# Routed attention: two small subtractions of each group are issued by VectorE instead of GpSimd

## Chip, cores and metric
One core of a Trainium2 chip (trn2). The metric is the device time of one execution, in microseconds (us); the median of three executions of the kernel before is 633.46 us.

## What is computed
The reference is a chain of six layers on a tensor of 32 images, 32 channels, 16x16 points (as tokens: 32 sequences of 256 tokens of width 32): linear attention, a peripheral convolution, a linear transformer, a mixture of experts, a squared attention, and at the end the routed blocks, which alone are touched here:

```python
def step(h, p):
    op = jnp.argmax(h[0, 0, :NOPS])
    q = h @ p['wq'][op]
    k = h @ p['wk'][op]
    v = h @ p['wv'][op]
    attn = jax.nn.softmax(jnp.einsum('bqd,bkd->bqk', q, k) * scale, axis=-1)
    y = jnp.einsum('bqk,bkd->bqd', attn, v) @ p['wo'][op]
    h = jnp.where(p['am'][op], y, h)
    z = jax.nn.relu(h @ p['w1'][op] + p['b1'][op]) @ p['w2'][op] + p['b2'][op]
    h = jnp.where(p['fm'][op], z, h)
    return (h, None)
```

The first value of the state decides which of 19 operations a step takes, and whether the step has an attention, a feed-forward part, both or neither. With these inputs the program runs three attentions in this stage.

## The kernel before
The kernel is one hand-written program with a stream of instructions for each engine; semaphores order them, and no scheduler moves anything. Within a stream the instructions run in the order of the code. The last stage is `routed_blocks` (from line 1510). A loop runs the steps that do something; `body(p)` is one step on each engine, written twice with two sets of semaphores (`sets[p]`).

**The attention of one step.** The 32 sequences are worked on in G = 8 groups of J = 4 sequences, which lie side by side in the 128 partitions. For a group g TensorE makes the scores twice. `scores` (line 1643) makes them with queries in the partitions, so that VectorE can take the maximum over the keys (`maximum`, L2085): one reduction for two of the group's sequences (`pair(0)` lies in PSUM banks 2 and 3, `pair(1)` in banks 0 and 1), 128 partitions x 1024 values to 4. `turned` (L1657) makes them with keys in the partitions, and ScalarE takes their exponential (L1909). The softmax needs the maximum of each query subtracted, and in the turned layout a query is a column. So the maxima are turned as well and brought in by a matmul (`shift`, L1651).

**The split.** The maxima are fp32, and they are turned and brought in as bf16. To lose no precision they are split in three parts. `m.parts` holds for each query 32 fp32 columns; `m.upper` is the same memory seen as pairs of bf16, and its index 1 is the upper half of each fp32 value. Part 0 is the maximum itself, part 1 is part 0 minus its own upper half, part 2 is part 1 minus its upper half. These two subtractions of 128x8 values are `split(g)` (L1977 and L1979 on GpSimd). Behind them TensorE turns the upper halves of all three (`maxima`, L1673, two transposes into PSUM), VectorE copies the result (`copy_maxima`, L2091; for group 0 it is ScalarE, L1896), and `shift` takes it from there.

**What waits for what.** `split(g)` waits for both maxima of group g (semaphore `max_done`), and its second subtraction for the first (`parts`). TensorE's `maxima(g+1)` waits for both subtractions of its group and also for the first maximum of the group after it, `maximum(g+2, 0)`, since the transposes are written into bank 2, which that maximum reads.

**The order on TensorE**, for group g: `pair_turned(g, 0)` (with the scores of pair 0 of group g+2 in between), `values(g-1)` (L1703), `pair_turned(g, 1)` (with the scores of pair 1 of g+2), `maxima(g+1)`, `sums(g-1)` (L1712, the denominators).

**The order on VectorE**, for group g: `maximum(g+2, 0)`, `spread_inverses(g-2)` (L2103), `copy_maxima(g+1)` (L2091), `invert(g-1)` (L2096 and L2098, which wait for the sums), `maximum(g+2, 1)`. So the maximum of pair 1 of one group stands directly in front of the maximum of pair 0 of the next. Ahead of the loop stand the four maxima of groups 0 and 1.

**The order on GpSimd**, for group g: `add_halves(g-1, 1)` (L1993, adds two halves of the exponentials for the sums), `split(g+1)`, `add_halves(g, 0)`, `normalise(g-2)` (L1984).

Of the kernel before, what the change touches and what calls it, by code (L numbers as in the profile page):

```python
# [8 lines left out]
ALU = mybir.AluOpType  # L9
# [1500 lines left out]
def routed_blocks(nc, m, sem):  # L1510
# [40 lines left out]
    def pair(h):  # L1551

        return (2, 3) if h == 0 else (0, 1)

    def scored(g, h):

        return 2 * g + h + 1
# [37 lines left out]
    def registers(eng, name):  # L1595
        return [eng.alloc_register(f"{name}_{r}") for r in ("step", "op", "code")]

    with nc.Block() as block:
# [364 lines left out]
        @block.gpsimd  # L1963
        def _(pool):
            regs = registers(pool, "pool")
            pool.memset(m.parts[:, :, :, :, :], 0.0).then_inc(zeroed, 1)
            pool.wait_ge(zeroed, 1)

            def body(p):
                sg, old = sets[p], sets[1 - p]  # L1970

                def split(g):

                    part = [m.parts[:, g % 2, :, :, 3 * g + i] for i in range(3)]
                    upper = [m.upper[:, g % 2, :, :, 3 * g + i, 1] for i in range(2)]
                    pool.wait_ge(sg["max_done"], scored(g, 1))
                    pool.tensor_tensor(part[1], part[0], upper[0], ALU.subtract).then_inc(sg["parts"], 1)  # L1977
                    pool.wait_ge(sg["parts"], 2 * g + 1)
                    pool.tensor_tensor(part[2], part[1], upper[1], ALU.subtract).then_inc(sg["parts"], 1)  # L1979

                def normalise(g):

                    pool.wait_ge(sg["inv_done"], g + 1)
                    pool.tensor_tensor(h[:, g * N:(g + 1) * N], m.yz[:, g, 0:N], m.yz[:, g, N:2 * N],  # L1984
                                       ALU.mult).then_inc(sg["y_made"], 1)

                def add_halves(g, i):

                    pool.wait_ge(sg["exp_done"], J * g + 2 * i + 2)
                    if g >= 2:  # L1990
                        pool.wait_ge(sg["sums_ready"], g - 1)
                    two = slice(2 * i, 2 * i + 2)
                    pool.tensor_tensor(m.esum[:, g % 2, two, :], m.et[:, g % 2, two, 0:N], m.et[:, g % 2, two, N:2 * N],  # L1993
                                       ALU.add).then_inc(sg["halves_added"], 1)

                def attention():
                    split(0)
                    split(1)
                    add_halves(0, 0)
                    for g in range(1, G):  # L2000
                        add_halves(g - 1, 1)
                        if g + 1 < G:
                            split(g + 1)
                            add_halves(g, 0)
                        if g >= 2:
                            normalise(g - 2)
                    normalise(G - 2)

                pool.wait_ge(old["through"], 3)
                for name in NAMES:  # L2010
                    pool.sem_clear(old[name])
                pool.sem_inc(cleared, 1)
                with pool.If(pool.snap(regs[2]) > 1):
                    attention()
                with pool.Else():
                    pool.nop()
                state(pool, "pool", regs, 1 - p)

            state(pool, "pool", regs, 0)
            in_turns(pool, regs, body)  # L2020

        @block.vector
        def _(dve):
# [45 lines left out]
            def body(p):  # L2069
                sg = sets[p]  # L2070

                def attention():
                    dve.wait_ge(sg["mats_ready"], 1)
                    dve.scalar_tensor_tensor(m.sabd[:, :], ps[:, 0, 0:128], float(C) ** -0.5, m.blkone[:, :],
                                             ALU.mult, ALU.mult).then_inc(sg["mats_masked"], 1)
                    dve.tensor_tensor(m.vobd[:, :], ps[:, 1, 0:128], m.blkone[:, :], ALU.mult).then_inc(sg["mats_masked"], 1)
                    candidates()
                    dve.wait_ge(zeroed, 1)

                    def maximum(g, h_):  # L2080
                        a = pair(h_)[0]
                        dve.wait_ge(sg["s_ready"], scored(g, h_))
                        if g >= 2:
                            dve.wait_ge(sg["m_ready"], g - 1)
                        dve.tensor_reduce(m.parts[:, g % 2, :, a:a + 2, 3 * g].rearrange("p s i -> p i s"),  # L2085
                                          ps[:, a:a + 2, :].rearrange("p i (s m) -> p i s m", s=S),
                                          AXX, ALU.max).then_inc(sg["max_done"], 1)

                    def copy_maxima(g):
                        dve.wait_ge(sg["m_ready"], g + 1)  # L2090
                        dve.tensor_copy(m.mrow[:, g % 2, :], m_ps(g)).then_inc(sg["m_copied"], 1)  # L2091

                    def invert(g):

                        dve.wait_ge(sg["sums_ready"], g + 1)
                        dve.transpose(m.sumt[:, :], ps[:, 6, N:2 * N]).then_inc(sg["sums_turned"], 1)  # L2096
                        dve.wait_ge(sg["sums_turned"], g + 1)
                        dve.reciprocal(m.sinv[:, :], m.sumt[:, 0:N:32]).then_inc(sg["sums_inverted"], 1)  # L2098

                    def spread_inverses(g):  # L2100

                        dve.wait_ge(sg["sums_inverted"], g + 1)
                        dve.transpose(m.yz[:, g, N:2 * N].rearrange("p (b c) -> p b c", c=32),  # L2103
                                      m.sinv[:, :].unsqueeze(2).broadcast_to([128, N // 32, 32])).then_inc(sg["inv_done"], 1)
                        if g == G - 1:
                            dve.wait_ge(sg["inv_done"], g + 1)
                            dve.wait_ge(sg["y_kept"], g + 1)
                            dve.tensor_tensor(h[:, g * N:(g + 1) * N], m.yz[:, g, 0:N], m.yz[:, g, N:2 * N],
                                              ALU.mult).then_inc(sg["y_last"], 1)

                    for g in range(2):
                        for i in range(2):
                            maximum(g, i)
                    for g in range(G):
                        if g + 2 < G:
                            maximum(g + 2, 0)
                        if g >= 2:
                            spread_inverses(g - 2)
                        if g + 1 < G:
                            copy_maxima(g + 1)  # L2120
                        if g >= 1:
                            invert(g - 1)
                        if g + 2 < G:
                            maximum(g + 2, 1)
                    spread_inverses(G - 2)
                    invert(G - 1)
                    spread_inverses(G - 1)

                def feed_forward():
                    dve.wait_ge(sg["loaded"], 16 * NLOAD)  # L2130
                    dve.wait_ge(sg["first_ready"], 1)
                    choose(1 - p, row=ps[0:1, 7, 64:64 + NOPS], read=sg["first_read"])

                    def relu(r):
                        dve.wait_ge(sg["z1_ready"], r + 1)
                        if r >= 4:
                            dve.wait_ge(sg["z2_ready"], (r - 4) // 2 + 1)
                        dve.tensor_scalar(hidden_pair(r), ps[:, up_pair(r), :], m.b1[:, p:p + 1], 0.0, ALU.add,  # L2138
                                          ALU.max).then_inc(sg["relu_v"], 1)

                    for r in RELU_V:
                        relu(r)
                    state(dve, "dve", regs, 1 - p)

                with dve.If(dve.snap(regs[2]) > 1):
                    attention()
                with dve.Else():
                    candidates()
                with dve.If(dve.snap(regs[2]) < 3):
                    feed_forward()  # L2150
                with dve.Else():
                    dve.wait_ge(sg["y_made"], G - 1)
                    dve.wait_ge(sg["y_last"], 1)
                    choose(1 - p)
                    state(dve, "dve", regs, 1 - p)
                dve.sem_inc(sg["through"], 1)
# [527 lines left out]
```

## Time and profile before
| | us |
|---|---|
| median of 3 executions | 633.46 |
| lowest, highest | 630.22, 634.5 |
| the profiled execution | 627.3 |
| its span, from first to last instruction | 625.5 |
| VectorE busy | 407.7 |
| TensorE busy | 538.3 |
| GpSimd busy | 157.7 |

The rows further down come from the profiled execution. PE is TensorE (PEld its weight loads), DVE is VectorE, ACT is ScalarE, POOL is GpSimd. A row of the timeline gives the start in us from the span's start, the duration in us, engine, line, operation, what is written and read, shapes and count; in brackets how long the engine sat idle before it and which instruction ended that. R names a large tile in which nearly all buffers of this stage lie, and ps is PSUM. "issue" means that the profile shows nothing that the engine waited for.

### The profile page before, as it was taken

How to read it: one execution, taken by the hardware profiler on the slowest of the kernel's cores; microseconds unless marked ns; L12 is line 12 of the kernel's file. 1: busy time of each engine (PE TensorE's matmuls, PEld its weight loads, DVE VectorE, ACT ScalarE, POOL GpSimd, SP SyncE). 2: the span in 40 equal slices, each digit the busy share in tenths (PEclk: the TensorE clock that was granted, in tenths of full speed). 3: DMA queues.
4: the chain of work that ended last, by engine and by line, in shares of the span. 5: the costliest groups of instructions: out<-in, count | busy, mean ns of one | idle time of the engine just before them, and what ended most of it. 6: DMA issues, size and time to landing. Idle time of an engine off the chain costs nothing. (4 is left out here: it accounts for less than half of the span.)

```text
span 625.5 us, 15132 instructions
## 1 busy us (share of the span) xinstructions
PE 538.3 (86%) x6151; PEld 324.8 (52%) x6156; DVE 407.7 (65%) x756; ACT 300.1 (48%) x511; POOL 157.7 (25%) x209
## 2 busy tenths in 40 slices
PE   7966879989999888787888879689998999899983
PEld 3555644659998632264655544326552654265420
DVE  5769886862224698786888858635765575568453
ACT  4157543233221300257888854354655465656562
POOL 1024520000000000404665600001770276038400
PEclk9768999999788889897999999768999999999987
DMA  8400042000000290000000000000000000000002
GB/s 242 44 2 3 4 166 57 2 1 1 1 1 0 45 209 18 2 2 1 3 2 1 3 19 1 9 11 2 2 2 12 1 2 1 12 1 2 1 6 70
DMA packets 21794, 15.05 MB, mean 24 GB/s; under 512 B 17209, under 2 KB 20313, under 8 KB 21082
## 3 DMA queue, kind: packets, MB, share of 16 engines
q1 hardware_dynamic: 21722, 14.00, 9.2%
q8 instruction: 56, 0.92, 0.6%
q14 instruction: 16, 0.13, 0.1%
HBM read 8.71 MB, written 1.08 MB: 16 GB/s over the span
## 5 line engine op out<-in xcount | busy, mean ns | idle before, releaser
L1909 ACT ACTIVATE R<-ps 128x512 f32<-128x512 f32 x96 | 52.1, 594 | 41.3 <-PE ps L1657 41.3
L2085 DVE TENSOR_REDUCE R<-ps 128x4 f32<-128x1024 f32 x48 | 56.5, 1209 | 11.6 <-PE ps L1643 11.3
L1436 POOL TENSOR_TENSOR R<-R 128x512 f32<-128x512 f32 x32 | 45.3, 1417 | 47.5 <-DVE R L1370 47.5
L1993 POOL TENSOR_TENSOR R<-R 128x512 f32<-128x512 f32 x42 | 53.3, 1268 | 15.7 <-ACT R L1909 15.7
L1370 DVE TENSOR_TENSOR R<-ps,lasting 128x512 f32<-128x512 f32 x64 | 41.2, 687 | 13.9 <-PE ps L1302 13.9
L1657 PE MATMUL ps<-tmpA,R 32*128 32x256 f32 x384 | 49.2, 374 | 0.0
L1643 PE MATMUL ps<-R,tmpA 32*128 32x256 f32 x384 | 48.4, 408 | 0.0
L1403 ACT ACTIVATE R<-R 128x1536 f32<-128x1536 f32 x32 | 47.3, 1477 | 0.1
L1302 PE MATMUL ps<-R,Q 32*128 32x128 f32 (+1 forms) x512 | 31.2, 358 | 14.9 <-ACT R L1419 14.9
L1302 PEld LDWEIGHTS ps<-R,Q 32*128 32x128 f32 x512 | 25.3, 192 | 22.5 <-DVE R L1370 19.0
L1657 PEld LDWEIGHTS ps<-tmpA,R 32*128 32x128 f32 x384 | 36.3, 185 | 1.0
L1977 POOL TENSOR_TENSOR R<-R 128x8 f32<-128x8 f32 x24 | 5.0, 206 | 122.4 <-DVE R L2085 122.4
L1789 PE MATMUL ps<-R,early 32*128 32x512 f32 x160 | 34.7, 760 | 0.0
L1932 ACT ACTIVATE R<-ps,b 128x1024 f32<-128x1024 f32 x25 | 27.0, 1113 | 10.0 <-PE ps L1789 10.0
L1643 PEld LDWEIGHTS ps<-R,tmpA 32*128 32x128 f32 x384 | 29.6, 189 | 4.0 <-ACT tmpA L1888 3.5
L1419 ACT ACTIVATE R<-ps 128x256 f32<-128x256 f32 x64 | 24.3, 380 | 12.8 <-DVE R L1370 12.8
L1225 POOL MEMSET R<- 128x512 bf16 x1 | 0.5, 524 | 112.7 <-POOLq L915 112.7
L1329 PE MATMUL ps<-R 128*32 128x128 f32 (+1 forms) x512 | 27.9, 338 | 1.1 <-ACT R L1403 1.0
L2138 DVE TENSOR_SCALAR R<-ps,b 128x1024 f32<-128x1024 f32 x15 | 19.3, 1284 | 14.6 <-PE ps L1789 14.2
L1703 PE MATMUL ps<-R,Q 128*32 128x256 f32 x384 | 25.7, 385 | 2.0 <-ACT R L1909 2.0
L89 PE MATMUL ps<-lasting 128*128 128x512 f32 x40 | 22.8, 723 | 2.7 <-DVE R L154 2.7
L1827 PE MATMUL ps<-R,early 128*32 128x512 f32 x160 | 23.0, 649 | 2.4 <-DVE R L2138 2.4
(328 smaller groups left out, 1154.9 us busy)
## 6 DMA issues: line engine op xcount, KB each, us to landing
R<-z SPq DMA_DIRECT2D x16, 256.0 KB, 5.0
R<-in_qv SPq DMA_DIRECT2D x1, 2560.0 KB
x<-in_x SPq DMA_DIRECT2D x4, 256.0 KB, 3.0
out<-x SPq DMA_DIRECT2D x4, 256.0 KB, 2.7
lasting<-in_lasting SPq DMA_DIRECT2D x1, 811.0 KB, 8.7
early<-in_early SPq DMA_DIRECT2D x1, 793.5 KB, 7.3
scatter<-in_scatter SPq DMA_DIRECT2D x1, 512.0 KB, 5.8
P<-scratch_w SPq DMA_DIRECT2D x16, 32.0 KB, 2.4
```

Source lines behind the costliest of these rows:

```text
L1302: mm = pe.matmul(ps[:, 2 * (u % 3) + k, s * N:N + s * 128], k_[rows, at:at + 128], m.qm[rows, h, at:(g + 1) * N], start=True, stop=True)
L1329: mm = pe.matmul(ps[rows_of(j), 6 + g % 2, s * 128:N], vm[:, (2 * g + s) * J + j, h, :], m.att[:, u % SLOTS, k, at:at + N - s * 128], star ...
L1370: dve.tensor_tensor(diagonal(u), ps[:, 2 * (u % 3):2 * (u % 3) + 2, :] .rearrange("p k (d n) -> p k d n", n=128)[:, :, 0:3:2, :], m.causal ...
L1403: act.activation(a, a, ACT.Silu, scale=1.0 / AHD).then_inc(act_done, 1)
L1436: pool.tensor_tensor(diagonal(u), diagonal(u), diagonal(u), ALU.mult).then_inc(diag_squared[1], 1)
L1643: return pe.matmul(ps[:, j, half * N:(half + 1) * N], ut[rows_of(j), at:at + 128], h[rows_of(j), cols], start=True, stop=True)
L1657: mm = pe.matmul(ps[:, turned_bank(g, j), t * N:(t + 1) * N], h[rows_of(j), at:at + 128], ut[rows_of(j), g * N:(g + 1) * N], start=False, ...
L1789: mm = pe.matmul(ps[:, 2 * (r % 3) + i, :], m.w1[p][rows_of(j), :], h[rows_of(j), k * CH:(k + 1) * CH], start=True, stop=True)
L1909: act.activation(m.et[:, g % 2, j, :], ps[:, turned_bank(g, j), :], ACT.Exp)\
L1932: act.activation(hidden_pair(r), ps[:, up_pair(r), :], ACT.Relu, bias=m.b1[:, p:p + 1])\
L1993: pool.tensor_tensor(m.esum[:, g % 2, two, :], m.et[:, g % 2, two, 0:N], m.et[:, g % 2, two, N:2 * N], ALU.add).then_inc(sg["halves_added" ...
L2085: dve.tensor_reduce(m.parts[:, g % 2, :, a:a + 2, 3 * g].rearrange("p s i -> p i s"), ps[:, a:a + 2, :].rearrange("p i (s m) -> p i s m", ...
```

## The change
`split(g)` moves word for word from GpSimd's stream to VectorE's. There it stands behind the second maximum of its group, once for each of the groups 0 and 1 ahead of the loop, and at the end of the turn of the loop for groups 2 to 7. Its waits are the same; VectorE now waits with them for itself.

```diff
-                def split(g):
-
-                    part = [m.parts[:, g % 2, :, :, 3 * g + i] for i in range(3)]
-                    upper = [m.upper[:, g % 2, :, :, 3 * g + i, 1] for i in range(2)]
-                    pool.wait_ge(sg["max_done"], scored(g, 1))
-                    pool.tensor_tensor(part[1], part[0], upper[0], ALU.subtract).then_inc(sg["parts"], 1)
-                    pool.wait_ge(sg["parts"], 2 * g + 1)
-                    pool.tensor_tensor(part[2], part[1], upper[1], ALU.subtract).then_inc(sg["parts"], 1)
-
...
                 def attention():
-                    split(0)
-                    split(1)
                     add_halves(0, 0)
                     for g in range(1, G):
                         add_halves(g - 1, 1)
                         if g + 1 < G:
-                            split(g + 1)
                             add_halves(g, 0)
...
+                    def split(g):
+
+                        part = [m.parts[:, g % 2, :, :, 3 * g + i] for i in range(3)]
+                        upper = [m.upper[:, g % 2, :, :, 3 * g + i, 1] for i in range(2)]
+                        dve.wait_ge(sg["max_done"], scored(g, 1))
+                        dve.tensor_tensor(part[1], part[0], upper[0], ALU.subtract).then_inc(sg["parts"], 1)
+                        dve.wait_ge(sg["parts"], 2 * g + 1)
+                        dve.tensor_tensor(part[2], part[1], upper[1], ALU.subtract).then_inc(sg["parts"], 1)
+
...
                     for g in range(2):
                         for i in range(2):
                             maximum(g, i)
+                        split(g)
                     for g in range(G):
...
                         if g + 2 < G:
                             maximum(g + 2, 1)
+                            split(g + 2)
```

The order of VectorE's instructions in the loop, one turn from copy to copy, before (the maxima are L2085, R is the tile with all buffers):

```order
L2091 COPY R<-ps 128x256
L2096 STREAM_TRANSPOSE R<-ps 128x256
L2098 RECIPROCAL R<-R 128x8
L2085 TENSOR_REDUCE R<-ps 128x2x2 x2
L2103 STREAM_TRANSPOSE R<-R 128x256
L2091 COPY R<-ps 128x256
```

And in the changed kernel (the maxima are L2073 there, the copy L2088):

```order
L2088 COPY R<-ps 128x256
L2093 STREAM_TRANSPOSE R<-ps 128x256
L2095 RECIPROCAL R<-R 128x8
L2073 TENSOR_REDUCE R<-ps 128x2x2
L2082 TENSOR_TENSOR R<-R 128x8
L2084 TENSOR_TENSOR R<-R 128x8
L2073 TENSOR_REDUCE R<-ps 128x2x2
L2100 STREAM_TRANSPOSE R<-R 128x256
L2088 COPY R<-ps 128x256
```

The two subtractions have come between the two maxima that stood side by side. On GpSimd a turn of the loop reads, before:

```order
L1993 TENSOR_TENSOR R<-R 128x512
L1977 TENSOR_TENSOR R<-R 128x8
L1979 TENSOR_TENSOR R<-R 128x8
L1993 TENSOR_TENSOR R<-R 128x512
L1984 TENSOR_TENSOR R<-R 128x256
```

There the subtractions stood between the two additions of halves, and these now follow each other.

## Rows read from the trace of the kernel before

**Rows 1.** The page: busy us, share of the span, number of instructions
```profile
PE 538.3 (86%) x6151; PEld 324.8 (52%) x6156; DVE 407.7 (65%) x756; ACT 300.1 (48%) x511; POOL 157.7 (25%) x209
```
**Rows 2.** Groups of instructions, 425 to 625 us: busy us, mean ns, idle before
```profile
L1977 POOL TENSOR_TENSOR R<-R 128x8 f32<-128x8 f32 x24 | 5.0, 206 | 122.4 <-DVE R L2085 122.4
L1979 POOL TENSOR_TENSOR R<-R 128x8 f32<-128x8 f32 x24 | 4.9, 206 | 1.9
```
**Rows 3.** Two stretches of one group each, by engine; then TensorE's granted clock
```profile
442.40:446.55 4.15, 4.15 (x66) 2.39 (x68) 3.52 (x7) 2.50 (x6) 2.89 (x6) 1.00 0.00 0
459.02:463.17 4.15, 4.15 (x50) 2.22 (x53) 2.40 (x5) 2.49 (x6) 3.58 (x7) 1.00 0.00 0
```
**Rows 4.** Waits, 425 to 625 us: total us, times, longest us
```profile
DVE R L2091 <- PE ps L1673: 18.6, 21, 2.4
PEld ps L1673 <- issue: 7.0, 21, 0.3
```
**Rows 5.** Timeline of VectorE in one group, with the two reductions apart
```profile
442.99 0.45 DVE L2096 STREAM_TRANSPOSE R<-ps 128x256 f32<-128x256 f32 x1 [0.31 <-PE ps L1712]
443.47 0.20 DVE L2098 RECIPROCAL R<-R 128x8 f32<-128x8 f32 x1
443.60 1.18 DVE L2085 TENSOR_REDUCE R<-ps 128x4 f32<-128x1024 f32 x1
444.69 1.22 DVE L2085 TENSOR_REDUCE R<-ps 128x4 f32<-128x1024 f32 x1
445.82 0.43 DVE L2103 STREAM_TRANSPOSE R<-R 128x256 f32<-128x256 f32 x1
446.55 0.29 DVE L2091 COPY R<-ps 128x256 bf16<-128x256 bf16 x1 [0.29 <-PE ps L1673]
```
**Rows 6.** Timeline: the weight loads of the transposes in that group
```profile
446.22 0.11 PEld L1673 LDWEIGHTS ps<-identb,R 128*128 128x128 bf16 x2 [0.33 <-issue]
```
**Rows 7.** Timeline: a copy that TensorE waits for, and its answer
```profile
438.35 0.29 DVE L2091 COPY R<-ps 128x256 bf16<-128x256 bf16 x1 [2.35 <-PE ps L1673]
438.69 0.10 PEld L1651 LDWEIGHTS ps<-R 32*128 32x128 bf16 x2 [0.56 <-DVE R L2091]
```
**Rows 8.** Timeline: the group with one reduction only
```profile
460.22 1.18 DVE L2085 TENSOR_REDUCE R<-ps 128x4 f32<-128x1024 f32 x1
462.85 0.11 PEld L1673 LDWEIGHTS ps<-identb,R 128*128 128x128 bf16 x2 [0.33 <-issue]
```
**Rows 9.** Timeline of GpSimd in the group of rows 5
```profile
443.33 1.27 POOL L1993 TENSOR_TENSOR R<-R 128x512 f32<-128x512 f32 x1 [0.92 <-ACT R L1909]
444.86 0.20 POOL L1977 TENSOR_TENSOR R<-R 128x8 f32<-128x8 f32 x1 [0.26 <-DVE R L2085]
445.14 0.21 POOL L1979 TENSOR_TENSOR R<-R 128x8 f32<-128x8 f32 x1
445.30 1.26 POOL L1993 TENSOR_TENSOR R<-R 128x512 f32<-128x512 f32 x1
```
**Rows 10.** Timeline of ScalarE: the two exponentials before GpSimd's second addition
```profile
444.14 1.08 ACT L1909 ACTIVATE R<-ps 128x512 f32<-128x512 f32 x2 [0.89 <-PE ps L1657]
```
**Rows 11.** Groups by shape, whole program: small operations of VectorE
```profile
L2407 DVE SCALAR_TENSOR_TENSOR shift<-bag,inv 128x8 f32<-128x8 f32 x1 | 0.2, 167 | 0.0
L2486 DVE TENSOR_TENSOR lasting<-lasting,ebpart 128x32 f32<-128x32 f32 x3 | 0.6, 192 | 0.1
```
**Rows 12.** Timeline of VectorE in the first groups of a pass
```profile
431.76 2.36 DVE L2085 TENSOR_REDUCE R<-ps 128x4 f32<-128x1024 f32 x2 [1.47 <-PE ps L1643]
434.77 1.23 DVE L2085 TENSOR_REDUCE R<-ps 128x4 f32<-128x1024 f32 x1 [0.66 <-PE ps L1643]
442.39 0.29 DVE L2091 COPY R<-ps 128x256 bf16<-128x256 bf16 x1 [1.28 <-PE ps L1673]
```
**Rows 13.** Timeline of VectorE: operations without a wait between them
```profile
473.79 0.13 DVE L2054 TENSOR_SCALAR state<-packed 1x1 int32<-1x1 int32 x1
473.85 0.13 DVE L2055 TENSOR_SCALAR state<-packed 1x1 int32<-1x1 int32 x1
```

## Prediction
> **What bounds the kernel now.** I read the busy times of the engines first [rows 1]. TensorE is busy for 538.3 us of 625.5, VectorE for 407.7 and GpSimd for 157.7, so over the whole program TensorE leads. The change lies in one stage only, the three passes of routed attention between about 428 and 591 us, so I then read the groups of instructions of that stage [rows 2]: the two subtractions stand there 24 times each, which is eight groups in three passes. GpSimd spends 5.0 + 4.9 us on them, and no row of the waits names them as what another engine waited for [rows 4].
>
> The share of busy time misleads here, so I read the stretches next. A stretch of one group, from one copy of the maxima to the next, lasts 4.15 us [rows 3]. TensorE is busy in all of it, and VectorE in 3.52 of it, which leaves it only about 0.6 us. In the stretch 459.02:463.17 VectorE has one reduction instead of two (2.40 us busy), and that stretch is no shorter. So TensorE sets this period, not VectorE, and its granted clock is 1.00, the upper of its two levels (2.4 GHz). The waits agree [rows 4]: VectorE waits for TensorE's transposes 21 times (18.6 us), and the weight loads of those transposes sit idle for a fixed 0.33 us each (7.0 us in 21) after "issue", with no engine named.
>
> The timeline of one group shows how much room VectorE's order has [rows 5]. Call the reduction of pair 1 A and the one that follows it, of pair 0 of the next group, B. A runs 443.60 to 444.78, B 444.69 to 445.91. TensorE's transposes of line 1673 wait for B, because they write over the scores that B reads, and start at 446.22 [rows 6]. How fast TensorE answers VectorE is seen where TensorE really is waiting: the copy at 438.35 ends at 438.64 and the weight load behind it starts at 438.69, 0.05 us later [rows 7]. So B could end at 446.17 without being felt. **The slack is 446.17 - 445.91 = 0.26 us.** That the 0.33 us in front of the transposes is no hidden wait for B is shown by the last group: at 462.85 the same transposes start after the same 0.33 us, with no B in front of them (the only reduction, at 460.22, had ended 1.45 us before) [rows 8].
>
> **What is removed, and what it gives.** GpSimd loses 48 subtractions, 9.9 us of busy time. In a group they stand between its two additions of halves [rows 9]: the first addition ends at 444.60, the subtractions run 444.86 to 445.35, the second addition starts at 445.30. The second addition needs two exponentials of ScalarE, which run 444.14 to 445.22 [rows 10]. GpSimd answers a release after 0.08 us (A ends at 444.78 and its first subtraction starts at 444.86 [rows 5, 9]), and 445.22 + 0.08 is 445.30. So the addition was not late, and removing the subtractions gives it nothing. After each pass GpSimd waits for VectorE's spread inverses, not for itself. I take the gain as 0. The waits bound it from above: no row has TensorE or ScalarE waiting for GpSimd at all.
>
> **What is added.** VectorE gets the two subtractions 24 times. None of its rows is this operation, so I take the nearest: a scalar_tensor_tensor of 128x8 takes 167 ns, a tensor_tensor of 128x32 takes 192 [rows 11], a reciprocal of 128x8 takes 0.20 us [rows 5]. I take 0.17 us, by the first, which has the same width and two tensor inputs. The change brings waits as well. The first subtraction waits for A's end, and the second for the first. What such a wait of VectorE on itself costs is seen at line 2098, which needs line 2096: the latter ends at 443.44 and the former starts at 443.47, 0.03 us later. B waits for nothing in the pair, and an operation without such a wait starts before its forerunner's end (A starts 0.13 us after the start of the reciprocal of 0.20 us, 0.07 early) [rows 5]. Worked out for the group of rows 5:
> A ends 444.78; first subtraction 444.81 to 444.98; second 445.01 to 445.18; B starts at 445.11 instead of 444.69. **B moves by 0.42 us and ends at 446.33.** TensorE starts the transposes at 446.38 instead of 446.22: **0.16 us late**, which is 0.42 less the slack of 0.26.
>
> What stands behind B: on VectorE the spread of the inverses (0.43 us) and then the copy of the maxima. The spread would end at 446.67. The copy waits for the transposes anyway, and it started 0.33 us behind their start (446.22 to 446.55 [rows 5, 6]), so it starts at 446.71, just behind the spread, and the spread adds nothing. The next group's matrix work waits for the copy and for the end of the sums, both of which move with the transposes. So the delay is passed on once for each group and not multiplied: TensorE's work after the transposes is unbroken until the next ones.
>
> How often it counts: B must be gated by a split and gate a transpose.
> - Groups 0 and 1, in front of the loop: VectorE is idle there anyway: two reductions run until 434.12, and the next, at 434.77, waits 0.66 us for TensorE [rows 12]. Two subtractions need about 0.4. In front of the earlier pair, at 431.76, the wait is longer (1.47 us). Nothing.
> - Group 2: VectorE is idle for 1.28 us before the copy at 442.39 [rows 12], so B's shift is absorbed. Nothing.
> - Groups 3, 4, 5, 6: in front of the copies at 446.55, 450.70, 454.86 and 459.02, of which the first stands in rows 5 as the pattern of all four. These count.
> - Group 7: no B behind it. Its subtractions would end at about 461.8, and the transposes that need them start at 462.85 [rows 8]. Nothing.
> That is 4 in each pass, 12 in all: 12 x 0.16 = **1.9 us more**. The fourth routed step has no attention, and neither this nor any stage ahead is touched. The profiled execution took 627.3 us with 625.5 of span, so it would take 629.2. The median of the runs before is 633.46 (630.22 to 634.5), 6.2 above the profiled one; the difference carries over as it is, since nothing in it hangs on this stage, and gives 635.4.
>
> The bounds of the unknown price: below, an operation without cost of waiting, as in two tensor_scalars of VectorE that start 0.06 us apart at 0.13 us each [rows 13]. That makes a step of 0.10 us for 0.17, a shift of 0.20, less than the slack, and 0 us. Above, GpSimd's own steps: 0.08 us behind the end of A (444.78 to 444.86) and 0.28 from the first subtraction to the second [rows 9], the second again 0.28 to B. Then B starts at 445.42, a shift of 0.73, 0.47 us late, 12 times: 5.6 us. I stay with 0.16, since the nearest rows are VectorE's own.
>
> **The rivals.**
> 1. *No change at all.* The two subtractions fit the slack, at the lower bound above. For it: the margin is small, 0.16 us out of 0.42. Against it: the 0.03 us at line 2098, and every wait costs VectorE the early start too. Time 633.5. Chance 0.22. The Trainium skill states the like in "VectorE: DVE Perf Modes", section "The DRAIN you can't avoid": there a semaphore behind each VectorE operation costs nothing over one behind the last alone. This trace does not bear it out for operations this short: with a wait 0.03 us lies between them, without one they overlap by about 0.07 to 0.09.
> 2. *The small operations cost VectorE what they cost GpSimd*, or the wait on its own reduction shows late. It decides where the step from one to the next exceeds 0.2 us. Place: between A and B, 12 times; price 0.3 to 0.47 us each, time 637 to 639. For it: the sources are strided and one is the bf16 upper half of the fp32 values. Against: a reciprocal of the same size takes 0.20 us, with 0.13 to the next start [rows 5]. Chance 0.13.
> 3. *Held up by GpSimd: clearly slower.* VectorE reads two SBUF tensors in the subtractions. If it could not do so while GpSimd's addition runs, a subtraction that meets one would wait up to 1.26 us. The subtractions would lie at 444.81 to 445.18, and GpSimd is between additions from 444.60 to 445.30 [rows 9], so they fit with 0.21 us in front and 0.12 behind. The mechanism decides only if they shift by more than that; once they do, VectorE waits for nearly the whole addition, 12 x (1.26 + 0.16) = 17 us, time 650. The Trainium skill has this rule in "SBUF — State Buffer", in its text on the shared port pair: an exclusive lock between a GpSimd operation that reads SBUF and a VectorE operation with two SBUF inputs. By the rule alone the sum would stay, as the gap in rows 9 shows. Chance 0.04.
> 4. *Faster*, by GpSimd's 0.5 us a group, if it were GpSimd's second addition that held the sums on TensorE. The additions end at 446.56 and the sums of that group follow a period later, and no wait names them [rows 4]. Four groups in three passes would give 6 us at most, time 627.5. Chance 0.01.
> The forecast itself has 0.60.
>
> **How the numbers follow.** About 1%, 6.3 us, is what a measurement of this kernel can tell from no change. Forecast, rival 1 and nearly all of rival 2 lie within it; slower by more is rival 3 and the upper end of rival 2 together with the spread of the median (0.04 + 0.03); faster by more is rival 4 and the spread (0.02). That gives 0.02, 0.91, 0.07. The range: below, no change less the spread of the runs shown, which reach 3.2 us under their median, 630.2; above, the upper bound of the price, 633.5 + 5.6 = 639.1. What it leaves out is rival 3, rival 4 and a median that strays further.
>
> **What would show each step.** On VectorE a pair of 128x8 subtractions of about 0.17 us, the first about 0.03 us behind A; 0.42 us more from A's start to B's in groups 3 to 6. TensorE's transposes about 0.16 us later behind their group's last matmul, and the period of a group 4.31 to 4.32 us instead of 4.15; the stretch with one reduction stays at 4.15. The VectorE busy time rises by about 8 us (48 x 0.17), GpSimd's falls by 9.9, TensorE's granted clock stays. The forecast is wrong if the period stays at 4.15 (rival 1), reaches 4.45 and more (rival 2), or if a subtraction starts only when an addition ends (rival 3).

## The result and the profile after

| | before | changed |
|---|---|---|
| median of 16 executions each, us | 633.43 | 637.27 |
| lowest, highest, us | 626.99, 636.8 | 634.53, 642.9 |
| ratio to before, 95% interval | | 1.0083 (1.0057 to 1.0108) |
| the profiled execution, us | 627.3 | 640.2 |

The changed kernel is slower, by 3.8 us between the medians and by 5.2 us (3.6 to 6.8) by the ratio. A second comparison of the same two programs (e6 below) gave a ratio of 1.0065 (1.0040 to 1.0089), or 4.1 us. The ratios leave out the slow executions, those more than 1.5% above the fastest of their kernel, so they need not be the ratios of the medians: two of the ten of e5 and three of the 29 beside e1 to e4 are such.

The two profiled executions differ by 12.9 us, but 8.6 of these arise before the routed attention starts (its first maximum starts at 436.55 instead of 427.93 us), in stages whose code is the same. The comparison is therefore made inside the routed stage.

The busy times of the engines, from the page of the changed kernel:

```profile
PE 547.7 (86%) x6151; PEld 330.1 (52%) x6156; DVE 416.4 (65%) x804; ACT 300.0 (47%) x511; POOL 149.1 (23%) x161
```

VectorE has 48 instructions and 8.7 us more than in [rows 1], GpSimd 48 instructions and 8.6 us less. (The forecast had 9.9 less, the sum of the 48 durations. Where a subtraction overlaps the addition behind it, by 0.05 us in [rows 9], the busy time loses less than that.) TensorE's busy time is 9.4 us longer with the same instructions, at a mean granted clock of 0.902 instead of 0.920 over the whole execution. The groups of instructions, 430 to 600 us, have the moved subtractions (busy us, mean ns):

```profile
L2082 DVE TENSOR_TENSOR R<-R 128x8 f32<-128x8 f32 x24 | 4.2, 176 | 0.8
L2084 DVE TENSOR_TENSOR R<-R 128x8 f32<-128x8 f32 x24 | 4.2, 175 | 0.8
```

They take 176 and 175 ns on VectorE where GpSimd took 206 [rows 2]. The timeline of one group answers rows 5, 6 and 9. L2073 is the maximum, L2082 and L2084 are the subtractions, L2100 the spread, L2088 the copy; the last rows are TensorE's transposes and GpSimd:

```profile
452.21 1.18 DVE L2073 TENSOR_REDUCE R<-ps 128x4 f32<-128x1024 f32 x1
453.43 0.18 DVE L2082 TENSOR_TENSOR R<-R 128x8 f32<-128x8 f32 x1
453.64 0.17 DVE L2084 TENSOR_TENSOR R<-R 128x8 f32<-128x8 f32 x1
453.73 1.22 DVE L2073 TENSOR_REDUCE R<-ps 128x4 f32<-128x1024 f32 x1
454.87 0.43 DVE L2100 STREAM_TRANSPOSE R<-R 128x256 f32<-128x256 f32 x1
455.41 0.29 DVE L2088 COPY R<-ps 128x256 bf16<-128x256 bf16 x1
455.07 0.13 PEld L1673 LDWEIGHTS ps<-identb,R 128*128 128x128 bf16 x2 [0.56 <-issue]
455.10 0.27 PE L1673 MATMUL ps<-identb,R 128*128 128x128 bf16 x2 [0.19 <-DVE R L2073]
453.92 1.27 POOL L1984 TENSOR_TENSOR R<-R 128x512 f32<-128x512 f32 x1 [0.70 <-ACT R L1909]
456.11 1.26 POOL L1984 TENSOR_TENSOR R<-R 128x512 f32<-128x512 f32 x1
458.32 1.27 POOL L1984 TENSOR_TENSOR R<-R 128x512 f32<-128x512 f32 x1 [0.95 <-ACT R L1909]
```

From the start of A to the start of B it is 1.52 us instead of 1.09. B ends at 454.95, and the weight load of the transposes starts at 455.07. Its idle time is now 0.56 us instead of 0.33, although the row still says "issue" (no cause that the profile shows); the row of the matmuls names VectorE's maximum. The waits of the stage, 430 to 600 us, show the same in total:

```profile
PEld ps L1673 <- issue: 9.7, 21, 0.6
PE ps L1673 <- DVE R L2073: 2.2, 12, 0.2
```

The second of these rows was not there before, and its count is the forecast one: 12. The first grew from 7.0 [rows 4] to 9.7 us, by 2.7 in 12. The stretches from copy to copy answer rows 3 (the last number but two is TensorE's granted clock):

```profile
455.41:459.80 4.39, 4.20 (x66) 2.40 (x68) 3.88 (x8) 2.50 (x6) 3.25 (x4) 1.00 0.01 4
468.60:472.75 4.15, 4.15 (x50) 2.23 (x52) 2.75 (x7) 2.26 (x6) 3.20 (x4) 1.00 0.00 0
```

A group of the four that count takes 4.39 to 4.40 us instead of 4.15 (one of the twelve 4.46). TensorE is busy for 4.20 of it and waits for the rest. The group without a B has stayed at 4.15. The granted clock is 1.00 in both. From the start of the first maximum of the first pass to the start of its last product (line 2108, L2105 now) it was 44.28 us and is 45.24: 0.96 more, or 4 x 0.24, so 2.9 us in three passes.

### The profile page after: what moved, and what is told of

Its sections match the earlier page's. It is cut to its first block and busy times, and to the rows that moved or that the text cites. A ratio compares the mean times of both kernels' runs of the same rounds, so it can differ in the third digit from the quotient of the medians.

```text
span 638.4 us, 15132 instructions
## 1 busy us (share of the span) xinstructions
PE 547.7 (86%) x6151; PEld 330.1 (52%) x6156; DVE 416.4 (65%) x804; ACT 300.0 (47%) x511; POOL 149.1 (23%) x161
## 5 line engine op out<-in xcount | busy, mean ns | idle before, releaser
L2073 DVE TENSOR_REDUCE R<-ps 128x4 f32<-128x1024 f32 x48 | 57.5, 1209 | 10.5 <-PE ps L1643 10.5
L2093 DVE STREAM_TRANSPOSE R<-ps 128x256 f32<-128x256 f32 x24 | 10.8, 450 | 20.3 <-PE ps L1712 13.9
```

## The experiments

Theory P is that of the prediction with its last term corrected: the whole cost lies between A and B in groups 3 to 6. Its rivals: that the mere presence of the subtractions in VectorE's stream costs something elsewhere (L), that GpSimd's additions hold VectorE up (rival 3 of the prediction), and that the longer pass also changes where TensorE's clock falls (D). "Period" is the distance between two copies of the maxima; the kernel before has 4.15 to 4.16 us in all but the first of each pass, which is 4.03 or 4.04 in every kernel. The edits are shown against the changed kernel.

**e1: only the four groups that count.** `split(3)` to `split(6)` on VectorE, the others on GpSimd. Not shown in the cut: GpSimd's own `split`, as in the kernel before, and a wait for the earlier parts where the engine changes.

```diff
+                    if 0 in (0, 1, 2, 7):
+                        split(0)
+                        split(1)
...
+                            if g + 1 in (0, 1, 2, 7):
+                                split(g + 1)
...
-                        split(g)
+                        if g in (3, 4, 5, 6):
+                            split(g)
...
-                            split(g + 2)
+                            if g + 2 in (3, 4, 5, 6):
+                                split(g + 2)
```

> Only the four subtraction pairs of groups 3 to 6 are on VectorE, those of groups 0, 1, 2 and 7 stay on GpSimd (with one more wait where the engine changes). Theory P (the cost lies between the two maxima of these four groups and nowhere else): the period from copy to copy in them is 4.39 to 4.40 us as in the changed kernel, each attention pass is 0.96 us longer than before, so 2.9 us over the kernel before, a ratio of 1.0046. Rival L (the changed kernel lost more than 2.9 us, its ratio being 1.0083, and the rest comes from something that the mere presence of the subtractions in VectorE's stream brings to the whole program): the ratio is between 1.003 and 1.008, and about half of the excess is gone with half of the instructions.

Measured: periods of 4.39 and 4.40 us (one of 4.47) in the twelve places, 4.15 and 4.16 in the last group; a pass of 45.25 us. The median of 6 executions was 640.12 against 632.12 us, ratio 1.0128 (1.0073 to 1.0183). The trace shows the changed kernel's delays in full with half of its instructions, as P has it. The ratio is above what both theories gave, from few executions; these also had a lower granted clock than those beside them, 0.9035 against 0.9104 in the mean (see behind e12).

**e2: the other four.** The same with groups 0, 1, 2 and 7 on VectorE.

> The complement: groups 0, 1, 2 and 7 on VectorE, where by the trace it is idle anyway, groups 3 to 6 on GpSimd. Theory P: period 4.15 to 4.16 us in all groups, passes as long as before, a ratio of 1.000. Rival L: half of the excess over 2.9 us remains, a ratio of 1.002 to 1.004 with periods of 4.15 us.

Measured: 632.79 against 632.12 us, ratio 1.0016 (0.9978 to 1.0054). VectorE's timeline in group 2, and the copy of group 3 as the last row (L2100 and L2102 are the subtractions, L2106 the copy):

```profile
443.20 1.21 DVE L2089 TENSOR_REDUCE R<-ps 128x4 f32<-128x1024 f32 x1
444.45 0.17 DVE L2100 TENSOR_TENSOR R<-R 128x8 f32<-128x8 f32 x1
444.66 0.18 DVE L2102 TENSOR_TENSOR R<-R 128x8 f32<-128x8 f32 x1
444.75 1.22 DVE L2089 TENSOR_REDUCE R<-ps 128x4 f32<-128x1024 f32 x1
447.04 0.29 DVE L2106 COPY R<-ps 128x256 bf16<-128x256 bf16 x1 [1.07 <-PE ps L1673]
451.19 0.29 DVE L2106 COPY R<-ps 128x256 bf16<-128x256 bf16 x1 [0.29 <-PE ps L1673]
```

In group 2 the subtractions have only shortened the idle time before the copy, from 1.28 [rows 12] to 1.07 us. The period is 4.15 or 4.16 in all groups but one (4.34). So the instructions cost nothing where VectorE waits anyway. With e1 this shows the place of the cost that the traces have. Rival L's 1.002 to 1.004 is not excluded by the interval; no period shows it.

**e3: three subtractions.**

```diff
-                        dve.wait_ge(sg["parts"], 2 * g + 1)
-                        dve.tensor_tensor(part[2], part[1], upper[1], ALU.subtract).then_inc(sg["parts"], 1)
+                        for k in range(2):
+                            dve.wait_ge(sg["parts"], 3 * g + 1 + k)
+                            dve.tensor_tensor(part[2], part[1], upper[1], ALU.subtract).then_inc(sg["parts"], 1)
```

TensorE's wait for `parts` goes with it, from `2 * (g + 1)` to `3 * (g + 1)`.

> In the changed kernel the second subtraction of each group is issued twice, each waiting for the one before, so VectorE's chain is 0.21 us longer. Theory P: no slack is left in groups 3 to 6, so all of it shows there: period 4.60 to 4.61 us, passes 1.8 us longer than before, 5.4 us in all (ratio 1.0086); nothing in groups 0 to 2 and 7. If instead TensorE's late answer (0.12 us rather than 0.05) is a fixed price of the change, the step from two to three subtractions still costs 0.21 us. If the delay were not passed on fully, the period stays under 4.5 us.

Measured: periods of 4.60 and 4.61 us at all twelve places, a pass of 46.08 us, so 5.4 us in three passes. The median was 636.02 against 632.12, ratio 1.0067 (1.0031 to 1.0103). The 0.21 us more between A and B come through in full, since the slack is gone.

**e4: one subtraction.**

```diff
-                        dve.wait_ge(sg["parts"], 2 * g + 1)
-                        dve.tensor_tensor(part[2], part[1], upper[1], ALU.subtract).then_inc(sg["parts"], 1)
```

TensorE waits for `g + 1` instead of `2 * (g + 1)` here. The third part of the maxima stays zero.

> The second subtraction of each group is left out, so the third part of the maxima stays zero. Theory P with TensorE answering after 0.12 us: the second maximum ends 0.22 us later than before, the slack is 0.26 - 0.07 = 0.19 us, so 0.03 us a group are left: period 4.18 us, 0.4 us in all (ratio 1.0006). With the answer after 0.05 us, as was forecast, the slack is 0.26 us and the period is 4.155 us, ratio 1.000. If the wait as such cost more than the time of the work, the period is 4.25 us or more.

Measured: periods of 4.18 and 4.19 us, ratio 1.0020 (0.9984 to 1.0055), 633.8 against 632.12 us. VectorE's timeline and the transposes:

```profile
451.93 1.19 DVE L2073 TENSOR_REDUCE R<-ps 128x4 f32<-128x1024 f32 x1
453.15 0.18 DVE L2082 TENSOR_TENSOR R<-R 128x8 f32<-128x8 f32 x1
453.24 1.22 DVE L2073 TENSOR_REDUCE R<-ps 128x4 f32<-128x1024 f32 x1
454.57 0.13 PEld L1673 LDWEIGHTS ps<-identb,R 128*128 128x128 bf16 x2 [0.35 <-issue]
```

B starts 1.31 us after A, 0.22 later than before, and ends at 454.46; TensorE answers 0.11 us later. The 0.03 us left over of a shift of 0.22 measure the slack: 0.19 us, not the 0.26 of the prediction. The changed kernel gives the same: 0.43 - 0.24 = 0.19. One, two and three subtractions give periods of 4.18, 4.40 and 4.61 us.

**e5: GpSimd kept busy.** An addition more on GpSimd, in front of the second addition of each group, with a semaphore `extra` of its own.

```diff
+                    if i == 1:
+                        if g >= 1:
+                            pool.wait_ge(sg["extra"], g)
+                        pool.tensor_tensor(m.relt[:, 0, :], m.et[:, g % 2, 3, 0:N], m.et[:, g % 2, 3, N:2 * N],
+                                           ALU.add).then_inc(sg["extra"], 1)
```

> The changed kernel, with one addition of 128x256 more on GpSimd (both operands in SBUF, result in a tile that nobody reads) in front of the second addition of halves of each group. It takes 0.73 us, so that GpSimd's addition of 1.27 us, which ended 0.46 us before VectorE's first subtraction, ends 0.25 to 0.3 us after the subtraction is due. Rival 3 of the prediction (VectorE cannot read two SBUF operands while GpSimd's addition runs): the first subtraction starts, or ends, 0.25 us or more later in groups 3 to 6, and their period grows from 4.40 to 4.6 us or more, 2.9 us in all. If the two engines do not hold each other up here: subtractions of 0.17 to 0.18 us, 0.03 us behind the maximum, period 4.40 us, and the time is the changed kernel's within 1 us.

Measured: 639.69 against 632.43 us between the medians, ratio 1.0075 (1.0045 to 1.0105), or 4.7 us (2.8 to 6.6). Two groups of the timeline, VectorE first, then GpSimd (L2087 and L2089 of VectorE are the subtractions, L1989 of GpSimd the additions of halves):

```profile
451.77 1.19 DVE L2078 TENSOR_REDUCE R<-ps 128x4 f32<-128x1024 f32 x1
452.99 0.52 DVE L2087 TENSOR_TENSOR R<-R 128x8 f32<-128x8 f32 x1
453.54 1.24 DVE L2089 TENSOR_TENSOR R<-R 128x8 f32<-128x8 f32 x1
458.79 0.24 DVE L2087 TENSOR_TENSOR R<-R 128x8 f32<-128x8 f32 x1
459.06 0.18 DVE L2089 TENSOR_TENSOR R<-R 128x8 f32<-128x8 f32 x1
452.19 2.56 POOL L1989 TENSOR_TENSOR R<-R 128x512 f32<-128x512 f32 x2
457.71 1.28 POOL L1989 TENSOR_TENSOR R<-R 128x512 f32<-128x512 f32 x1
```

The two subtractions that take 0.18 us each took 0.52 and 1.24 where GpSimd's two additions ran without a break from 452.19 to 454.75: the first ended at 453.51, when GpSimd's first addition had ended (452.19 + 1.27 = 453.46), and the second at 454.78, when the second had (454.75). In the next group the first subtraction took 0.24 us, until 459.03, with GpSimd's addition until 458.99. So the mechanism of rival 3 is real: in this trace a subtraction of two SBUF operands on VectorE does not finish while such an addition runs on GpSimd, and nearly the whole addition can stand in front of it. VectorE's reduction from PSUM is not held up so: in the changed kernel it took its 1.22 us from 453.73, beside GpSimd's addition from 453.92. The period was 5.80 and 5.81 us in group 3 of each pass, and 4.44 to 4.46 in groups 4 to 6, 7.6 us more than in the kernel before in all. The expected 4.6 us for these was too high, since the additions overlapped by 0.06 us and not by 0.25. The Trainium skill has it as an exclusive lock ("SBUF — State Buffer", the text on the shared port pair), and this trace agrees. In the changed kernel the lock does not bite: all 48 subtractions took between 173 and 179 ns. In the group shown they ran from 453.43 to 453.81, between two additions on GpSimd that ended at 453.22 and started at 453.92.

**e6 and e7: both kernels once more.** No edit.

> The changed kernel once more, beside the kernel before on the same chip. Theory P alone (12 delays of 0.24 us): 2.9 us over the kernel before, ratio 1.0046, periods of 4.40 us. Theory D (besides, the longer pass shifts where TensorE's clock falls to the lower level at the start of the second and third pass, 1.6 us each time; in the trace of before it fell at one of the two, in those of the changed kernel and of e1 at both): ratio 1.007 to 1.008 and the distance from a pass's last copy to the next pass's first copy 35.6 us at both places.

> The kernel before, as a measurement of nothing, which shows what this kind of comparison gives for no change: ratio 1.000 with an interval that holds it, periods of 4.15 us, and by theory D at most one of the two distances between passes at 35.6 us, the other at 34.0 us.

Measured: e6 637.02 and e7 632.19 against 632.43 us, ratios 1.0065 (1.0040 to 1.0089) and 1.0004 (0.9973 to 1.0034). Periods as in the first traces, 4.39 to 4.41 and 4.15 to 4.16. From the last copy of a pass to the first of the next it was 35.52 and 35.63 us in e6, and 33.89 and 35.70 in e7. In the first traces it was 35.53 and 35.64 in the changed kernel, and 35.57 and 33.99 in the kernel before.

**e8: two of the four groups.** As e2, with groups 3 and 4 on VectorE as well.

> As e2, and also the subtractions of groups 3 and 4 on VectorE, so two of the four groups that count. Theory P: periods of 4.40 us for two groups of each pass and 4.15 for the others, passes 0.48 us longer, 1.4 us in all (ratio 1.0023). If the four groups were not independent (a delay that only shows when several follow each other), the two would give less than 0.24 us each.

Measured: periods of 4.40 us in the two and of 4.15 or 4.16 in the others, a pass of 44.76 us; so each group costs its 0.24 whether or not the later ones do. The time was 632.84 against 632.43 us, ratio 0.9990 (0.9962 to 1.0018), less than the 1.0023 that the trace accounts for.

**e9: TensorE's two waits in the other order.**

```diff
-                    pe.wait_ge(sg["parts"], 2 * (g + 1))
                     if 1 <= g < G - 1:
                         pe.wait_ge(sg["max_done"], scored(g + 1, 0))
+                    pe.wait_ge(sg["parts"], 2 * (g + 1))
```

> The changed kernel with the two waits of TensorE in front of the transposes in the other order, first for the maximum, then for the subtractions (which are done earlier). In all traces so far TensorE answers the maximum after 0.11 to 0.12 us, where the prediction had taken 0.05 from a copy. If the late answer comes from the place of the wait (the last wait sits on the instruction itself, the one before it is an instruction of its own), it changes with the order: 0.05 us and a period of 4.33, or more than 0.12. If it belongs to this pair of instructions, period 4.40 and 0.12 us stay.

Measured, in one execution: periods of 4.32 and 4.33 us at all twelve places. B and the transposes:

```profile
456.07 1.22 DVE L2073 TENSOR_REDUCE R<-ps 128x4 f32<-128x1024 f32 x1
457.34 0.12 PEld L1673 LDWEIGHTS ps<-identb,R 128*128 128x128 bf16 x2 [0.50 <-DVE R L2073]
```

B ends at 457.29 and the weight load starts 0.05 us later, not 0.11 to 0.12. The row now names VectorE as the releaser. So 0.07 us of each of the twelve delays hung on the order of two waits in the source, of which the one for the subtractions had been satisfied more than 1 us before. That is 0.8 us of the 2.9 by the trace; one execution (636.83 us, and 636.39 for the changed kernel beside it, e10) cannot show it in the whole time. The answer of 0.05 us that the prediction read [rows 7] has this order too: in `shift` the wait for the copy is followed by one for an exponential (`exp_done`).

**e10, e11, e12: more traces for theory D.** The changed kernel, the kernel before and e8, one execution each.

> A third trace of the changed kernel, for the distances between passes. Theory D: again 35.5 to 35.6 us at both. Otherwise one of them at 33.9 to 34.0.

> A third trace of the kernel before. Theory D: again exactly one of the two distances at 35.6 us and one at 34.0 us. Otherwise none or both.

> A second trace of e8. In its first both distances were long, 35.5 and 35.6 us, and yet its runs lay only 0.7 us over those of the kernel before, where twelve delays would be six and give 1.4 us. Theory D (where the clock falls follows from the length of the pass) wants both long again; if they differ from look to look of the same kernel, the place is left to chance and D cannot carry the rest of the changed kernel's loss.

Measured: e10 35.53 and 35.64 us, e11 33.90 and 35.69, e12 35.53 and 35.62. The 1.6 us lie in the first matmuls of a pass. In the kernel before, at the start of the second and third pass (timeline):

```profile
483.52 2.97 PE L1724 MATMUL ps<-R 128*128 128x512 f32 x4 [0.38 <-DVE R L2074]
486.43 1.80 PE L1643 MATMUL ps<-R,tmpA 32*128 32x256 f32 x16
543.97 1.98 PE L1724 MATMUL ps<-R 128*128 128x512 f32 x4 [0.38 <-DVE R L2074]
545.88 1.16 PE L1643 MATMUL ps<-R,tmpA 32*128 32x256 f32 x16
```

And in the changed kernel:

```profile
493.06 3.62 PE L1724 MATMUL ps<-R 128*128 128x512 f32 x4 [0.38 <-DVE R L2062]
554.48 3.63 PE L1724 MATMUL ps<-R 128*128 128x512 f32 x4 [0.38 <-DVE R L2062]
```

The stretches around them, of the changed kernel:

```profile
488.50:492.50 4.00, 2.67 (x22) 0.86 (x20) 1.28 (x1) 2.33 (x3) 0.00 (x0) 1.00 0.08 13
492.50:496.50 4.00, 3.62 (x6) 1.17 (x4) 2.85 (x5) 0.60 (x1) 0.00 (x0) 0.57 0.02 4
554.00:558.00 4.00, 3.62 (x5) 1.17 (x4) 2.85 (x5) 0.60 (x1) 0.00 (x0) 0.57 0.02 4
```

and of the kernel before, for the second and for the third pass:

```profile
479.00:483.00 4.00, 2.62 (x20) 0.79 (x20) 1.28 (x1) 2.26 (x3) 0.00 (x0) 1.00 0.05 5
483.00:487.00 4.00, 3.62 (x10) 1.35 (x12) 2.85 (x5) 1.06 (x2) 0.00 (x0) 0.67 0.02 4
539.00:543.00 4.00, 2.56 (x21) 0.47 (x18) 1.28 (x1) 2.49 (x3) 0.00 (x0) 1.00 0.07 9
543.00:546.00 3.00, 2.62 (x12) 1.19 (x14) 2.35 (x4) 0.61 (x2) 0.00 (x0) 1.00 0.02 5
```

Four matmuls take 1.98 us at a granted clock of 1.00 (2.4 GHz) and 3.6 where the mean is 0.57, so mostly at the lower level (1.2 GHz). The idle time ahead does not tell the two cases apart: TensorE was idle for 1.3 to 1.4 of the 4 us ahead of the falls, and for 1.4 of 4 ahead of the third pass of the kernel before, where the clock stayed.

A distance of 35.5 to 35.7 us (long) has a fall, one of 33.9 to 34.0 has none. All traces and whole times together, the times by the ratio; the delays are those of the trace inside the passes:

| kernel | delays, us | long distances of two | whole time over the kernel before, us |
|---|---|---|---|
| before (three traces) | 0 | 1, 1, 1 | e7: 0.3 (-1.7 to 2.2) |
| changed (three traces) | 2.9 | 2, 2, 2 | 5.2 (3.6 to 6.8), e6: 4.1 (2.5 to 5.6) |
| e1 | 2.9 | 2 | 8.1 (4.6 to 11.6) |
| e2 | 0.2 | 1 | 1.0 (-1.4 to 3.4) |
| e3 | 5.4 | 1 | 4.2 (2.0 to 6.5) |
| e4 | 0.4 | 1 | 1.3 (-1.0 to 3.5) |
| e5 | 7.6 | 0 | 4.7 (2.8 to 6.6) |
| e8 (two traces) | 1.4 | 2, 2 | -0.6 (-2.4 to 1.1) |
| e9 | 2.1 | 1 | one execution |

A longer pass does not as such mean more falls: e3 and e5 have longer passes than the changed kernel and one and none. With 1.6 us added for a second long distance and taken off for none, the sums for the changed kernel (4.5) and e5 (6.0) lie inside their intervals, where the delays alone miss one of the two for the changed kernel and that for e5; e1's 4.5 lies just under its interval. But e8 would be 1.4 + 1.6 = 3.0 us or 1.0047, and its interval ends at 1.0018. (Its runs lay 0.4 us over those beside them between the medians, not the 0.7 of the expectation.)

The mean granted clocks of the timed executions that the ratios use also speak on this. In the 35 of the kernel before in the comparison of e5 to e8, the five shortest have 0.914 and 630.3 us in the mean, and the five longest 0.903 and 635.8. e1, which lies above its trace, had a lower clock than the executions beside it (0.9035 against 0.9104); e3 and e5, which lie below theirs, a higher one (0.9138 against 0.9104, and 0.9128 against 0.9077). In these three what the whole time shows beyond the trace goes with the clock. For the changed kernel it does not: e6 has 0.9093 against 0.9077, where a further fall as in the rows above would lower the mean by about 0.003 (an estimate: 4 us at 0.57 instead of 1.00, out of 637). So D holds for the traces taken, and is not shown for the timed executions.

## Why the prediction was right, and where it was short

- **What bounds the stage, and where the change counts.** Right. Twelve places and no others: the counts in the waits (12), e1 and e2. The granted clock stayed at 1.00 in these stretches, but not over the whole execution, which the prediction did not separate.
- **Nothing is gained on GpSimd.** Right. Its additions now follow 0.70 and 0.95 us of waiting for ScalarE, where the subtractions stood.
- **The shift of B.** Forecast 0.42 us, measured 0.43 (1.52 less 1.09). The subtractions took 0.18 where 0.17 was taken, and each stood 0.03 to 0.04 us behind what it waited for. The nearest rows of VectorE, not GpSimd's, were the right ones to take.
- **The slack.** This is the term that was mis-sized. It was worked out as 446.17 less 445.91, with an answer of TensorE after 0.05 us that was read at a different instruction, the weight load behind a copy. At the transposes the answer takes 0.11 to 0.12 us, so the slack is 0.19 (e4), and each group pays 0.24 instead of 0.16: 2.9 us instead of 1.9. e9 shows that the two numbers differ by the order of the waits, for with the other order the answer takes 0.05 us and the period is 4.32 to 4.33, where 4.31 to 4.32 was forecast.
- **The delay is passed on once for each group.** Right: 0.21 us more between A and B give 0.21 us more in the period (e3), and two groups give twice 0.24 (e8).
- **The range, 630.2 to 639.1, and the chances.** The median of 637.27 lies within, nearer the upper end than the forecast of 635.4; the change is slower by less than 1%, as 0.91 had it, although the ratio's interval reaches 1.0108. That the time lies so well inside is in part luck. The upper end came from GpSimd's prices for the two subtractions (0.47 us a group), which VectorE did not pay, and it had no term for the 1.2 to 2.3 us that the passes do not explain.
- **Rival 1 (no change)** fell by the 0.03 us of each wait and the lost early start of B. **Rival 2** fell by its price: from one subtraction to the next it was 0.21 us, at the 0.2 from which it was to decide, but each group pays 0.24 and not 0.3 or more, and no period reached 4.45. **Rival 3** fell in this kernel, but its mechanism exists (e5); the gap on GpSimd keeps it away. **Rival 4** fell, as no time was gained.
- **What stays open.** The traces account for 2.9 us within the passes. The two comparisons gave 5.2 (3.6 to 6.8) and 4.1 us (2.5 to 5.6). The rest, 1.2 to 2.3 us, would be filled in the main by one more fall of TensorE's clock between passes, as all three traces of the changed kernel have it; e8 and the mean clocks of e6 speak against taking that as settled. Its cause is not shown. The stages ahead, in which the clock also differs from execution to execution, were not followed.

## What to carry over

When work moves to an engine that looks idle, look at where in its order the idle time lies: the same two instructions cost nothing in four groups and 0.24 us each time in the other four. Work out the slack with the answering time of the very instruction that will wait, since 0.07 us were nearly half of the forecast delay of 0.16. Where two kernels differ by less than the spread of one, compare the granted clocks of the executions too, before the rest of a difference is put down to the edit. Where an instruction waits for two semaphores, it is worth trying which of the two waits is written last.

## What had not been expected of the hardware

- TensorE answered the same semaphore after 0.11 to 0.12 us with the wait for it written directly before the transposes, and after 0.05 us with the other, satisfied wait between (e9, and [rows 7] for another pair). With the late answer the profile writes "issue" as the reason of the idle time of the weight load; with the early one it names VectorE.
- A VectorE subtraction of 128x8 with both operands in SBUF took 0.52 and 1.24 us instead of 0.18 while GpSimd added 128x512 in SBUF (e5). It is its duration that grows in the trace, and not an idle time before it, so the waits do not show it.
- TensorE's granted clock fell at the start of some passes, at 1.6 us each time. In three traces of the changed kernel and in two of e8 it fell at the same places; in the kernel before it fell at one of the two, and not always the same one. TensorE had been busy for about two thirds of the 4 us ahead, where the clock fell and where it did not.
